# Issuing the third pair of stack loads with the first two, ahead of the last two batches' stores

## The reference, cut to what matters

```
x = x + L0_xattn(layernorm(x), ctx, ctx, mask)     # 16 heads of 16, masked softmax
x = x + L0_ffn(layernorm(x))                       # self-attention, then 8 experts, the best one per token
x = x + L1_xattn(layernorm(x), ctx, ctx)           # 16 heads of 16
x = x + L1_ffn(layernorm(x))                       # 8 experts, the best one per token
```

```
q, k, v = split_heads(X @ Wq), split_heads(Y @ Wk), split_heads(Y @ Wv)
attn = softmax(q k^T / sqrt(16)) v ;  out = merge_heads(attn) @ Wo
```

## Time and profile before

| what | us |
|---|---|
| median of 3 runs | 1257.46 |
| lowest and highest run | 1255.79 and 1257.50 |
| the profiled execution, its own time | 1255.79 |
| its span in the profile | 1254.0 |
| TensorE busy | 1113.0 |
| VectorE busy | 837.7 |
| ScalarE busy | 645.2 |

### The profile page before, as it was taken

How to read it: one execution, slowest core, us unless ns; L and a number is a source line. 1 busy time by engine, 2 the same in 40 slices (tenths; PEclk the granted TensorE clock), 3 DMA queues, 4 the chain that set the end, 5 groups by cost and what they waited for, 6 DMA issues and landing times. The chain is left out here.

```text
span 1254.0 us, 17668 instructions
## 1 busy us (share of the span) xinstructions
PE 1113.0 (89%) x5550; PEld 538.4 (43%) x5578; DVE 837.7 (67%) x2112; ACT 645.2 (51%) x1341; POOL 211.2 (17%) x273
## 2 busy tenths in 40 slices
PE   7889999999897999999868999996979999998390
PEld 4423343334453233333365666664523333335370
DVE  5888777777478899898671222123789988876732
ACT  3446666666543676667713333331527767675250
POOL 3310000000143000000203122211520010102154
PEclk9989999999999899999968999998979999999795
DMA  8953212220048443432391041103883422201064
GB/s 256 318 177 106 81 48 51 85 52 1 1 170 285 110 109 95 129 100 69 97 356 38 27 164 31 28 10 103 268 268 78 106 60 78 72 11 59 28 174 143
DMA packets 102867, 139.40 MB, mean 111 GB/s; under 512 B 11188, under 2 KB 84792, under 8 KB 101368
## 3 DMA queue, kind: packets, MB, share of 16 engines
q1 hardware_dynamic: 98696, 128.04, 33.2%
q0 software_dynamic: 4080, 10.23, 3.1%
HBM read 86.30 MB, written 52.17 MB: 110 GB/s over the span
## 5 line engine op out<-in xcount | busy, mean ns | idle before, releaser
L889 ACT ACTIVATE r<-ps 128x512 f32<-128x512 f32 x768 | 428.0, 600 | 213.1 <-PE ps L975 124.0
L377 DVE TENSOR_REDUCE m<-ps 128x1 f32<-128x512 f32 x512 | 320.4, 682 | 36.6 <-PE ps L962 36.5
L975 PE MATMUL ps<-r 99*128 99x512 bf16 x768 | 292.9, 387 | 12.3 <-DMA r<-mT 6.3
L962 PE MATMUL ps<-r 96*128 96x512 bf16 x720 | 282.2, 393 | 14.2 <-DVE m L377 5.5
L989 PE MATMUL ps<-r 128*32 128x512 f32 x1536 | 205.0, 606 | 5.8 <-ACT r L889 3.3
L373 DVE CUSTOM_DVE_ANT_0 r<-ps,r 128x512 bf16<-128x512 f32 x256 | 170.0, 690 | 53.8 <-PE ps L962 53.1
L975 PEld LDWEIGHTS ps<-r 99*128 99x128 bf16 x768 | 74.4, 98 | 221.2 <-ACT r L889 157.9
L962 PEld LDWEIGHTS ps<-r 96*128 96x128 bf16 x720 | 71.0, 99 | 99.4 <-DVE m L377 27.1
L865 POOL COPY r<-r 128x256 f32<-128x256 f32 x48 | 19.0, 400 | 527.6 <-PE ps L989 527.6
L1662 DVE COPY r<-ps 128x512 f32<-128x512 f32 x46 | 31.8, 691 | 90.3 <-PE ps L1709 90.3
L657 PE MATMUL ps<-r,w 128*128 128x512 f32 x192 | 89.0, 601 | 0.5 <-issue 0.5
(11 more groups left out here) (152 smaller groups left out, 1192.3 us busy)
## 6 DMA issues: line engine op xcount, KB each, us to landing
r<-q_parts SPq DMA_DIRECT2D x48, 384.0 KB, 4.2
r<-k_parts SPq DMA_DIRECT2D x48, 384.0 KB, 5.1
k_parts<-r SPq DMA_DIRECT2D x24, 384.0 KB, 3.3
q_parts<-r SPq DMA_DIRECT2D x24, 384.0 KB, 3.2
r<-in_w SPq DMA_DIRECT2D x16, 512.0 KB, 3.5
r<-in_w SPq DMA_DIRECT2D x8, 1024.0 KB, 14.9
k_parts<-r SPq DMA_DIRECT2D x24, 256.0 KB, 3.2
q_parts<-r SPq DMA_DIRECT2D x24, 256.0 KB, 3.2
```

Source lines behind the costliest of these rows:

```text
L377: ins = dve.tensor_reduce(out, mem.ps[:, bank, :], AX.X, ALU.max)
L889: act.activation(mem.probs[:, u // HG, u % HG, :], ps[:, ST + (UNITS * g + u) % DEEP, :], ACT.Exp, scale=SCALE).then_inc(a.p_exp.sem, 1)
L962: pe.matmul(ps[:, led_bank(n), :], mem.qst[g][0:ROWS, h, t * P:(t + 1) * P], mem.kst[g][0:ROWS, h, :], start=True, stop=True).then_inc(a.s ...
L975: ins = pe.matmul(out, mem.kst[g][0:KROWS, h, kt * P:(kt + 1) * P], mem.qst[g][0:KROWS, h, :], start=True, stop=not a.masked)
```

## The change

In `rest_of_batches` of `project_sync` the loop that loads the stacks before the last two batches' stores runs over AHEAD groups instead of AHEAD - 1, and the separate load of group 2 after those stores goes.

```
         for n in range(QK):
             sp.wait_ge(a.stored[n].sem, a.stored[n].at(1))
-        for g in range(AHEAD - 1):
+        for g in range(AHEAD):
             load_stacks(sp, a, 0, g)
         body(B - 2, None)
         body(B - 1, None)
-        load_stacks(sp, a, 0, AHEAD - 1)
```

## The result

The change makes the kernel slower: 1265.12 us (1263.40 to 1267.07, 6 runs) against 1257.06 us (6 runs of the kernel before), a ratio of 1.0064, 95% interval 1.005 to 1.0079, which is 6.3 to 9.9 us. A second measurement, beside the experiments further down, gave 1.0067 (1.0048 to 1.0085). The forecast was slower by 3.4 us, and its range ended at 1263.5. The direction held and the size did not.

The account below looks back on a forecast made before the run. TensorE, busy 1113.0 of 1254.0 us, was taken to set the time, so DMA order acts only where it waits. Delays 7.9 less gains 4.5 gave +3.4 us, 1260.9 us; range 1252.7 to 1263.5, the forecast's own 1256.4 to 1262.5.

Parts of the forecast that it names:

- Where the change acts: L589 waits for `k_parts` in all stages, SyncE goes from last store to shift, `mT` wait falls from 1.9 to 0.4 us.
- signs of being wrong: Store's landing time unchanged, `mT` wait as long as before, or granted clock of 0.50 in the middle of batch 3's projection.
- The delay: Third load ahead of batch 2's stores delays batch 3's first block: 3.1 + 1.7 + 3.1 = 7.9 us over three stages.
- The slack of sa0: In sa0 L589 waited for TensorE, the store landing 1.4 us earlier, so the delay there is 1.7 us.
- What the prediction drew from it for the stores: By the completion-order rule, the stores' semaphores would land behind the added load's writes.
- The gain: Load gone from ahead of the shift: 1.5 us for each stage, 4.5 us gained over three.
- the upper bound of 1.85 us: At the shift, VectorE's maxima in sa0 limit the useful earlier start of TensorE to 1.85 us a stage.
- the whole 1.85 would be gained: At the shift, by the completion-order rule: 1.85 us gained in each stage, making the sum +2.4 us.
- The clock: Rival: TensorE's new gap in xa0 and xa1 halves the clock, +18 us, 1279 us with the rest; chance 0.06.
- The prediction had put it at nothing: Everything in the change besides the stores' delay and the shift's gain was said to cost nothing.
- The loads were not hidden: Rival: batch 2's block 0 store lands as before, shifts start 1.5 us sooner, 1253.0 us; chance 0.20.
- no mixture of rates made gain and loss equal: Rival: mixed loads and stores exceed 255 GB/s, delays 5.2 us against gains 5.1, time stays 1257.6; chance 0.14.

Follow-up runs that it names:

- The doubled load: The change plus a fourth 768 KB load behind the third, ahead of batch 2's stores, its data unused; against the kernel before: 1.0139 (1.0117 to 1.0162).
- where it stands alone, the one between: Group 2's load placed between the stores of batch 2 and batch 3, against the kernel before: 0.9974, and 0.9965 the second time.
- sa0 alone: Third load early in stage sa0 only, xa0 and xa1 as in the kernel before; against that kernel: 1.0028 (1.0014 to 1.0041), +3.5 us.
- the gap filled for its first half: The change plus twelve extra matmuls in TensorE's gap in batch 3's projection, against the kernel before: 1.0042 (1.0024 to 1.006).
- the kernel with the delay alone: The change with group 2's load made once more at its old place, ahead of the shift; against the kernel before: 1.0078 (1.0058 to 1.0098), 9.9 us.

## Why the prediction was wrong

- **Where the change acts: right.** ScalarE's L589 waits for `k_parts` in all three stages, SyncE goes from the last store to the shift, and the wait for `mT` is gone, where 0.4 us had been expected to stay. But one of the prediction's own signs of being wrong is there as well: a granted clock of 0.50 in the middle of batch 3's projection, in xa1.
- **The delay: right as a sum, 7.9 forecast and 8.1 measured** (2.57, 2.01, 3.56; in the second profile 3.06, 1.43, 3.60). The doubled load adds 3.2 us a pair in the mean. The closeness of the sum has some luck in it, since the stages were forecast at 3.1, 1.7 and 3.1. The slack of sa0, 1.4 us, was there: the store lands 3.36 us later against the first L657 of batch 3, the remainder comes 2.01 later. By the Trainium skill (DMA: Bandwidth & Descriptors, "Queues, rings and completion order") a DMA's semaphore write lands only after every earlier write of the same DMA engine. What the prediction drew from it for the stores agrees, as far as 9.50 us to landing instead of 8.23 can show it.
- **The gain: mis-sized, 4.5 forecast, 3.65 in the change's profile, 3.3 and 4.4 where it stands alone.** The step that failed is the upper bound of 1.85 us for a stage, and the 1.5 taken from it: TensorE's first transposed score may start early, but the score behind it waits for VectorE's last maximum, so 0.70 us of gap remains and the bound is 1.14 in sa0. TensorE's first start came 2.1 us sooner, of which the kernel kept about half. The prediction drew from the same rule of the Trainium skill that the whole 1.85 would be gained. For the landing the trace agrees: in sa0 TensorE starts 1.85 us after the last DMA of the shift is issued, where it took 2.69. The rule says nothing of the score behind.
- **The clock: the step that failed most.** I made it a rival with a chance of 0.06 and a price of 18 us, on the ground that a gap of 1.75 us at 44 us had left the clock at 1.00. In xa0 and sa0 the gaps were 1.73 and 1.59 us in the change (2.23 in xa0's second profile), and the clock held. In xa1 the gap was 3.25 us, 3.31 in the second profile, and it fell in both. I had taken some 2 us for both xa0 and xa1, and not seen that in xa1 VectorE already waited 0.87 us for ScalarE before the change, so that gap and delay add. The price was 2.0 us in one stage and not 9, since the clock was back after one block and a half.
- **The sum.** 8.14 - 3.65 + 2.0 = 6.5 us, and the starts lost 7.2 in the same profile. Of the difference 0.8 lies in xa0, between VectorE's 13th maximum and the second copy to `mT` (8.62 us against 7.85): there the clock rose later after the start, at 83.1 us in place of 80 us. In the second profile the same sum is 8.1 - 3.9 + 1.9 = 6.1 and the starts lost 8.5; the other 2.5 us all lie in that stretch (8.73, 7.73 and 7.90 us in the three stages, against 7.85, 7.43 and 6.58). The prediction had put it at nothing. Whether it is the change's doing is open; another kernel whose xa0 is as before also had the longer time, 8.59 us. So some 6.1 to 6.5 of the 8.1 us are accounted for by causes that were tested. Also open is the 3.5 us of sa0 alone.
- **The rivals.** The loads were not hidden, and no mixture of rates made gain and loss equal. Without the clock the two measured terms give 8.14 - 3.65 = 4.5 us, 1262 us, inside the range. The range failed because it took the clock as a case by itself and far away, where it was a smaller term of the likeliest case.

## What to carry to other kernels

A transfer moved out of the way of one wait lands in front of another: look for the first consumer behind its new place, and price it with the engines' rate for that very kind of transfer. Of three places for one load, the old one costs some 4 us and the early one 12 against the one between. And a bound on a gain must be read at each instruction behind the one that starts earlier, not only at that one; a new gap on TensorE must be priced with its clock, by its full length, what was idle there already included, and as a term of the forecast, not only as a rival.

## What was unexpected of the hardware

- Windows of 2 us with stack loads show 238 to 268 GB/s with all DMA engines occupied, windows of stores 370 to 406. The doubled load cost the line behind it 3.2 us in the mean for 768 KB, which is about this rate (2.7 us in sa0, 4.0 in xa0).
- The granted clock stayed at 1.00 through gaps of TensorE of 1.59, 1.73 and 2.23 us and fell after one of 3.25 us and, with half of the load early, one of 2.53. But with the gap filled for its first half it fell after the 1.83 us that were left, and in the kernel with the delay alone it fell after 1.98 us in xa0 and held through 1.99 us in sa0. So the length of a gap alone doesn't tell.
- Twenty extra matmuls a stage, useless in themselves, held the clock at 1.00 over the three starts once the load stood between the stores, and that kernel took 0.7% less time than before, 0.35% of it by the load's place. The same twenty brought no gain that can be told where a wait of 1.98 us followed them.
